# Attention by pairs of query tiles with transposed scores, on one Trainium2 core

## The chip, the cores and the metric

One NeuronCore of a Trainium2 chip runs one program. The metric is the device time of that program in microseconds (us). Engines are called as in the profile: PE (TensorE), PEld (its weight loads), DVE (VectorE), ACT (ScalarE), POOL (GpSimd), SP (SyncE).

## The reference

Two samples of 1024 tokens with 256 features, in two layers; x is (2, 1024, 256).

```
layer 0:  w[b]  = normalised(mix_weight * cond[b])             # 256x256 for each sample
          x     = x + tanh((w[b] mixed x) @ W @ A1 @ A2 + bias)
layer 1:  Q2 = x @ Wq2 + bq2;  K2 = x @ Wk2 + bk2;  V = [cond, x] @ Wv + bv
          A  = softmax(Q2 @ K2.T / 16) - alpha * softmax(constant rows)
          att = A @ V                                           # (2, 1024, 256)
          xq = fake_quant(att);  h = fake_quant(silu(xq @ Wg.T) * (xq @ Wu.T))
          x  = x + h @ Wd.T                                     # int8-like weights, I = 704
```

The second softmax has equal scores in each row, so the kernel replaces it by a rank-one term. `fake_quant` needs the largest magnitude of the whole attention output, so the FFN can't start before the last attention tile is done.

## The kernel before

All matmuls up to the attention are made of three fp32r passes over a high and a low half of each operand (`three_passes`, L1001): high by high, high by low, low by high. Every operand therefore exists as two tiles (`xh`/`xl` the projected queries, `x1h`/`x1l` the tokens that serve as keys, `vh`/`vl` the values, `pth`/`ptl` the probabilities). ACT writes the high half by a copy to fp32r, DVE or POOL the low half by a subtraction (`low`, L593).

The queries are projected by Wq2 Wk2^T at once, so scores are a product of `xh`/`xl` with the tokens themselves. The attention runs over 16 query tiles j of 128 queries (8 a sample). For each tile, in the order in which PE's program lists them (loop at L1247):

- `scores(j)`, L1127: queries on partitions, 1024 keys along two PSUM banks, 12 matmuls of 512 columns. Two pairs of banks alternate (0/1 and 2/3).
- `out_T(j-3)`, L1186: two transposes that bring an output tile back to feature-major form.
- `attend(j-2)`, L1155: 24 matmuls of 256 columns; the transposed probabilities are the weights, the values are the moving operand.
- single items of other work (`extra`, `do_extra`, L1212): 6 query projections of 6 matmuls each, 4 value tiles, transposes of the FFN weights.
- `prob_T(j-1)`, L1143: 8 transposes of 128x128, since the product with V needs keys on partitions.

Meanwhile DVE takes the row maximum of a tile (`row_max`, L733) and ACT makes the exponential straight from PSUM with the maximum as its bias and the row sum as its accumulator (`softmax`, L463). After `prob_T`, ACT copies the high half of the transposed tile (`probT_hi`, L473) and DVE makes the low half (`probT_lo`, L744). DVE scales the result by the reciprocal sum (`attention_out`, L750), PE transposes it back, ACT writes `outT` (`out_hi`, L480) and DVE takes its maximum (`out_max`, L759). POOL does no attention work; it quantises the FFN weights (L951 to L962), with scales that DVE makes in six turns (`ffn_weight_scales`, L764).

Before the loop PE runs 12 of the 16 value tiles with `scores(0)` and `scores(1)` between them (L1225), then `rank_columns` (L1237). PSUM bank 7 (`MISC`) is passed from item to item in the order of `misc_schedule` (L53); `misc_turn` (L1171) makes PE wait until the item before has been read. Every engine executes its program strictly in order. After the last tile PE waits for the maximum over all tiles and spreads it (`spread_max`, L1293, L1298), and the FFN begins.

Of the kernel before, what the change touches and what calls it, by code (L numbers as in the profile page):

```python
# [22 lines left out]
P = 128  # L23
# [8 lines left out]
NG = NH  # L32
IF = I // P
# [19 lines left out]
def misc_schedule():  # L53

    extra = {}
    for g in range(1, NG):  # L60
        for c in range(DC):
            extra[4 * (g - 1) + 1 + c] = [("query", g, c)]
    extra[1].insert(0, ("rank", 0))
    for j, v in ((3, 12), (4, 13), (7, 14), (8, 15)):
        extra[j] = [("value", v)]
    extra[11], extra[12], extra[13] = [("gate", 0)], [("gate", 1)], [("up", 0)]
    order = []
    for j in range(NT):
        if j >= 3:
            order.append(("out", j - 3))  # L70
        order += extra.get(j, [])

    order += [("out", NT - 3), ("out", NT - 2), ("out", NT - 1), ("down", 0), ("down", 1), ("up", 1)]
    return extra, order


def build_block(nc, x, cond, mix_w, l0_w, l0_a1, l0_a2, l0_bias, wq1, bq1, wq2, bq2, wk1, bk1, wk2, bk2,
                wv, bv, alpha, clip_x, clip_down, w_gate, w_up, w_down, out):
    extra, misc_order = misc_schedule()
    misc_at = {item: n for n, item in enumerate(misc_order)}  # L80

    def misc_reads(item):


        return sum(i[0] not in ("query", "value", "rank") for i in misc_order[:misc_at[item] + 1])
# [15 lines left out]
    def sums(u):  # L101
# [14 lines left out]
              (3, 4, "act", "act")]  # L116

# [8 lines left out]
    with ExitStack() as ctx:  # L126
# [42 lines left out]
        prob = sb("prob", [P, 2, L], F32)  # L169
        pth = sb("pth", [P, 2, TPB, P], F32R)  # L170
# [32 lines left out]
        with ExitStack() as scope:  # L203
# [4 lines left out]
            vh = sb("vh", [P, NT, D], F32R, scope)  # L208
            vl = sb("vl", [P, NT, D], F32R, scope)
# [5 lines left out]
            with ExitStack() as inner:  # L215
                ptl = sb("ptl", [P, 2, TPB, P], F32R, inner)
# [13 lines left out]
        MISC = 7  # L230
        own_bank = {("out", NT - 1): 6, ("down", 0): 4, ("down", 1): 5, ("up", 1): 7}

        def attended(j):
            return ps[:, 6, (j % 2) * D:(j % 2 + 1) * D] if j < NT - 1 else ps[:, 3, 0:D]

        def probT_bank(j, a):
            return a + (4 if j < NT - 1 else 0)

        EARLY_V = 12
# [49 lines left out]
        s_ps, nb_ready, p_ready = sem("s_ps"), sem("nb_ready"), sem("p_ready")  # L289
        t_ps, pth_ready, ptl_ready = sem("t_ps"), sem("pth_ready"), sem("ptl_ready")  # L290
# [29 lines left out]
        def hidden(u):  # L320
            i, t = units[u]
            return hid[:, i, t:t + L] if i < IF else hidr[:]

# [51 lines left out]
        def _(act):  # L375
# [75 lines left out]
            def query_hi(g, c, src):  # L451
                act.activation(xh[:, g // 2, c, half(g)], src, ACT.Identity, bias=col("ucol", c)).then_inc(qh_ready, 1)
# [7 lines left out]
            def value_hi(v, bank):  # L460
                copy(vh[:, v, :], ps[:, bank, 0:D], vh_ready)

            def softmax(j):  # L463
                act.wait_ge(nb_ready, j + 1)
                if j >= 2:
                    act.wait_ge(t_ps, 2 * (j - 1))
                if j >= 4:
                    act.wait_ge(o_ready, j - 3)
                act.activation(prob[:, j % 2, :], ps[:, 2 * (j % 2):2 * (j % 2) + 2, :], ACT.Exp,  # L469
                               bias=col("nb", j % 2), scale=ATT_SCALE,  # L470
                               accum_out=col("ls", j % 4)).then_inc(p_ready, 1)

            def probT_hi(j):  # L473
                for a in range(2):
                    act.wait_ge(t_ps, 2 * j + a + 1)
                    if j >= 2:
                        act.wait_ge(o_ps, j - 1)
                    copy(pth[:, j % 2, a * 4:(a + 1) * 4, :], ps[:, probT_bank(j, a), :], pth_ready)

            def out_hi(j):  # L480
# [916 lines left out]
```

## Time and profile before

| | |
|---|---|
| median of 3 runs | 244.15 us (243.93 to 244.63) |
| the profiled execution | 243.51 us, span 241.4 us, granted clock 0.983 |
| busy, share of the span | PE 94%, PEld 77%, DVE 63%, ACT 50%, POOL 29% |
| chain that ended last | PE 77%, DVE 13%, issue 3%, DMA 3%, ACT 2%, POOL 1% |
| attention stage | 57 to 191 us of the span |
| FFN and output | 191 to 241 us of the span |

The span runs from the first to the last instruction; 2.1 us of the profiled execution lie around it. Busy shares are averages over stages with different limits. Matmuls overlap, so the time that one costs is read from the starts of two neighbours and not from its duration. A granted clock of 1.0 is TensorE's 2.4 GHz, 0.5 is 1.2 GHz.

### The profile page before, as it was taken

The page shows a single profiled execution, that of the slowest core. Times are in us where ns is not written, and L with a number is a line of the kernel's source. Part 1 is how long each engine was busy: PE and PEld are TensorE (multiplying, and loading weights), DVE is VectorE, ACT ScalarE, POOL GpSimd, SP SyncE. Part 2 cuts the span into 40 slices and gives each one's busy share as a digit, 9 for nine tenths or more (in the row PEclk, how much of TensorE's full clock was granted, in tenths as well). Part 3 has the DMA queues.
Part 4 walks back from the last instruction along what each step waited for, and adds up shares of the span by engine and source line. Part 5 has one row for each costly group of instructions (what it writes and reads, how often), then busy time and mean ns, then how long its engine had stood idle before and what let it go on. Part 6 is the DMA issues. An engine that isn't in the chain of part 4 may idle for free.

```text
span 241.4 us, 3860 instructions
## 1 busy us (share of the span) xinstructions
PE 227.7 (94%) x1447; PEld 185.2 (77%) x1447; DVE 152.8 (63%) x328; ACT 120.9 (50%) x218; POOL 69.5 (29%) x95
## 2 busy tenths in 40 slices
PE   7379899999999999999999999999999999998994
PEld 7169799988997999989999998889999644433342
DVE  0772434687475568756876566455556497999963
ACT  2517442675334434443444534555436669944932
POOL 5265240433000000380572500000000065673750
PEclk9959999999999999999999999999999999999998
DMA  5980006600000000000000000000000000000044
GB/s 149 380 298 3 0 0 181 204 1 0 3 0 0 3 0 0 3 1 1 3 0 0 3 0 0 3 1 0 3 0 1 3 0 0 3 0 0 0 170 177
DMA packets 6817, 9.61 MB, mean 40 GB/s; under 512 B 768, under 2 KB 4880, under 8 KB 6800
## 3 DMA queue, kind: packets, MB, share of 16 engines
q1 hardware_dynamic: 6192, 8.59, 10.5%
q10 hardware_dynamic: 288, 0.79, 0.9%
q8 instruction: 11, 0.18, 0.3%
q0 software_dynamic: 320, 0.01, 0.1%
q14 instruction: 6, 0.05, 0.1%
HBM read 7.28 MB, written 2.10 MB: 39 GB/s over the span
## 4 chain that ended last, share of the span: by engine, by line
PE 77%; DVE 13%; issue 3%; DMA 3%; ACT 2%; POOL 1%; DVEq 0%; POOLq 0%
PE ps L1007 53%; PE ps L1151 6%; DVE hmax L851 4%; PE ps L1334 3%; PE ps L991 3%; DMA wl<-in_L_cond_weight 3%; PE ps L1286 2%; DVE hid L846 2%; PE ps L1036 1%; PE ps L1191 1%; PE ps L1360 1%; PE ps L999 1%; DVE wmix L622 1%; POOL hid L970 1%; DVE hi L893 1%
## 5 line engine op out<-in xcount | busy, mean ns | idle before, releaser
L1007 PE MATMUL ps<-vh,pth 128*128 128x256 f32 x128 | 37.4, 292 | 0.3 <-DVE ptl L594 0.3
L1007 PE MATMUL ps<-vl,pth 128*128 128x256 f32 x128 | 36.1, 282 | 0.0
L1007 PE MATMUL ps<-vh,ptl 128*128 128x256 f32 x128 | 36.1, 282 | 0.0
L469 ACT ACTIVATE prob<-ps,small 128x1024 f32<-128x1024 f32 x16 | 17.8, 1115 | 21.7 <-DVE small L741 21.7
L484 ACT ACTIVATE outT<-ps,small 128x128 f32<-128x128 f32 x32 | 10.0, 366 | 33.3 <-PE ps L1191 33.3
L1007 PE MATMUL ps<-x1h,xh 128*128 128x512 f32 x64 | 26.2, 409 | 0.0
L739 DVE TENSOR_REDUCE small<-ps 128x1 f32<-128x1024 f32 x16 | 19.6, 1222 | 10.1 <-PE ps L1007 9.9
L1007 PE MATMUL ps<-x1h,xl 128*128 128x512 f32 x64 | 25.2, 393 | 0.0
L1007 PEld LDWEIGHTS ps<-vh,pth 128*128 128x128 f32 x128 | 24.4, 191 | 0.9 <-issue 0.9
L1007 PE MATMUL ps<-x1l,xh 128*128 128x512 f32 x64 | 25.0, 390 | 0.0
L1007 PEld LDWEIGHTS ps<-vl,pth 128*128 128x128 f32 x128 | 24.5, 191 | 0.0
L1007 PEld LDWEIGHTS ps<-vh,ptl 128*128 128x128 f32 x128 | 24.4, 191 | 0.0
L594 DVE TENSOR_TENSOR ptl<-ps,pth 128x512 fp32r<-128x512 f32 x32 | 20.3, 679 | 4.6 <-ACT pth L383 4.6
L966 POOL CAST xq<-xi 128x512 bf16<-128x512 int8 x5 | 3.7, 774 | 57.4 <-DVE xi L830 57.4
L756 DVE TENSOR_SCALAR on_s<-ps,small 128x256 f32<-128x256 f32 x16 | 7.8, 485 | 18.2 <-issue 14.3
L383 ACT ACTIVATE pth<-ps 128x512 fp32r<-128x512 f32 x32 | 17.2, 598 | 1.4 <-PE ps L1151 1.2
L943 POOL TENSOR_TENSOR x1l<-x1T,x1h 128x512 fp32r<-128x512 f32 x8 | 10.1, 1280 | 25.4 <-ACT x1h L383 25.4
L1151 PE MATMUL ps<-ident,prob 128*128 128x128 f32 x128 | 16.6, 274 | 0.0
L1151 PEld LDWEIGHTS ps<-ident,prob 128*128 128x128 f32 x128 | 14.5, 141 | 0.8
L958 POOL TENSOR_SCALAR wgn<-wgn,winv 128x256 f32<-128x256 f32 x6 | 2.9, 479 | 39.5 <-DVE winv L772 39.5
L1007 PEld LDWEIGHTS ps<-x1h,xl 128*128 128x128 f32 x64 | 12.0, 188 | 2.7
L541 ACT ACTIVATE sil<-ps,gus 128x1024 f32<-128x1024 f32 (+1 forms) x12 | 12.4, 1046 | 3.1 <-PE ps L1286 3.1
(224 smaller groups left out, 549.9 us busy)
## 6 DMA issues: line engine op xcount, KB each, us to landing
result<-yst SPq DMA_DIRECT2D x8, 256.0 KB, 2.1
xn<-in_x SPq DMA_DIRECT2D x3, 512.0 KB, 8.8
wdn<-in_L_ffn_w_down SPq DMA_DIRECT2D x1, 704.0 KB, 7.4
wgn<-in_L_ffn_w_gate SPq DMA_DIRECT2D x1, 640.0 KB, 4.4
wun<-in_L_ffn_w_up SPq DMA_DIRECT2D x1, 640.0 KB, 5.3
xn<-in_x ACTq DMA_DIRECT2D x1, 512.0 KB, 8.4
a<-in_L_ffn_aux_weight SPq DMA_DIRECT2D x2, 256.0 KB, 8.6
wvf<-in_L_cond_Wv SPq DMA_DIRECT2D x1, 512.0 KB, 9.4
```

The lines of the kernel that those rows point to most:

```text
L383: act.activation(dst, src, ACT.Copy).then_inc(ready, 1)
L469: act.activation(prob[:, j % 2, :], ps[:, 2 * (j % 2):2 * (j % 2) + 2, :], ACT.Exp, bias=col("nb", j % 2), scale=ATT_SCALE, accum_out=col( ...
L484: ins = act.activation(outT[:, c, j * P:(j + 1) * P], ps[:, own_bank.get(("out", j), MISC), c * P:(c + 1) * P], ACT.Identity, bias=col("rc ...
L541: act.activation(sil[:, u % 4, s], flat(ps[:, 4 * (u % 2):4 * (u % 2) + 2, :])[:, s], ACT.Silu, scale=gus[:, units[u][0]:units[u][0] + 1]) ...
L594: dve.tensor_tensor(dst, src, hi.bitcast(F32), ALU.subtract).then_inc(ready, 1)
L739: link(dve.tensor_reduce(col("mx", j % 2), flat(ps[:, 2 * (j % 2):2 * (j % 2) + 2, :]), X_AXIS, ALU.max))
L756: dve.tensor_scalar(on_s[:, j % 2, :], attended(j), col("rl", j % 2), None, ALU.mult).then_inc(o_ready, 1)
L851: dve.tensor_reduce(hmax[:, u:u + 1], hidden(u), X_AXIS, ALU.max, apply_absolute_value=True).then_inc(hm_ready, 1)
L943: pool.tensor_tensor(x1l[:, n // 2, c, half(n)], x1T[:, n, c, :], x1h[:, n // 2, c, half(n)].bitcast(F32), ALU.subtract).then_inc(x1l_read ...
L991: last = pe.matmul(ps[:, bank, m * D:(m + 1) * D], aT[:, k, m * P:(m + 1) * P], b[:, k, :], start=(k == 0), stop=(k == DC - 1))
L1007: last = pe.matmul(dst, a, b, start=(n == 0), stop=(n == len(passes) - 1))
L1151: last = pe.transpose(ps[:, probT_bank(j, a), k * P:(k + 1) * P], prob[:, j % 2, (4 * a + k) * P:(4 * a + k + 1) * P], ident[:])
```

## The change

Query tiles are taken in 8 pairs g of 256 queries, and the scores are computed transposed.

- PE: `scores(g)` has keys on partitions. For each of 8 key tiles, 6 matmuls with the tokens as weights and 256 queries as columns; banks 0 to 3 hold one pair. There is no second set of banks, so each bank waits for the reader of the pair before. `prob_T` is gone. The values carry two columns of ones, so `attend` has 258 columns and yields the sum of the probabilities itself.
- The maximum of a query lies now across partitions and banks: DVE reduces over key tiles (`key_max`, two reductions that read PSUM in steps of 256 elements, and one maximum), PE transposes the result (`key_max_T`), DVE finishes it (`query_max`), and PE spreads it over all partitions (`spread_top`). Both PE steps stand inside `attend(g-1)`, ahead of its matmul 15 of the first tile and matmul 3 of the second.
- `distances(g)`: DVE subtracts the maximum from the scores in four pieces of 512 into `prob`, of which there is one only. ACT makes the exponential in place and then copies the high half, piece by piece. POOL makes the low halves of pieces 0 to 2, DVE that of piece 3; in the last pair POOL makes piece 0 and DVE the others.
- All 16 values, `rank_columns` and the first query projection stand before `scores(1)`. The output of a pair is transposed by four transposes (`out_T`) in the middle of `scores(g+2)`.
- The FFN weights are scaled by DVE in pairs 1 to 3, quantised by POOL after its low halves, and transposed by PE in pairs 4 to 6 and ahead of the last `attend`.

The core of the diff (all else in it is renaming, semaphores and the split of POOL's weight loop):

```diff
+QP = 256
+NP = TOK // QP
+PPB = L // QP
...
+            after_scores[2 * (g - 1) + c] = ("query", g, c)
+    after_attend = {4: ("gate", 0), 5: ("gate", 1), 6: ("up", 0)}
+    order = [("rank", 0), after_scores[0], after_scores[1]]
+    for g in range(2, NP):
+        order.append(("out", g - 2))
+        order += [t[g] for t in (after_scores, after_attend) if g in t]
+    at_end = [("up", 1), ("out", NP - 2), ("down", 0), ("down", 1), ("tile", 0), ("tile", 1)]
+    return after_scores, after_attend, at_end, order + at_end
...
+    def low_half_on(g, k):
+        return "dve" if k == 3 or (g == NP - 1 and k > 0) else "pool"
...
-        prob = sb("prob", [P, 2, L], F32)
-        pth = sb("pth", [P, 2, TPB, P], F32R)
+        prob = sb("prob", [P, TPB, QP], F32)
+        pth0 = sb("pth0", [P, TPB, QP], F32R)
...
+                ptl = sb("ptl", [P, 2, TPB, QP], F32R, inner)
+        pth = [pth0, xh[:, 1].rearrange("p c n -> p (c n)").rearrange("p (k q) -> p k q", k=TPB)]
+        maxima = downT.rearrange("p i d -> p (i d)").bitcast(F32)
+        kmax = maxima[:, 0:2 * QP].rearrange("p (h q) -> p h q", h=2)
+        qmax = maxima[:, 2 * QP:3 * QP]
...
-        EARLY_V = 12
+        MISC, MAXB = 7, 6
+        own_bank = {("up", 1): 1, ("down", 0): 2, ("down", 1): 3, ("tile", 0): MAXB, ("tile", 1): 0}
+        def value_bank(v):
+            return (6, 7, 4, 5)[v] if v < 4 else (5, 7, 4)[v % 3]
...
+            def softmax(g):
+                for k in range(4):
+                    act.wait_ge(d_ready, 4 * g + k + 1)
+                    act.activation(prob[:, 2 * k:2 * k + 2, :], prob[:, 2 * k:2 * k + 2, :], ACT.Exp,
+                                   scale=ATT_SCALE).then_inc(p_ready, 1)
+                    if k == 0 and g >= 2:
+                        act.wait_ge(o_ps, 2 * (g - 1))
+                    act.wait_ge(p_ready, 4 * g + k + 1)
+                    copy(pth[g % 2][:, 2 * k:2 * k + 2, :], prob[:, 2 * k:2 * k + 2, :], pth_ready)
...
+            for v in range(NT):
                 act.wait_ge(v_ps, v + 1)
...
+                value_hi(v, value_bank(v))
+            extra_read(after_scores[0])
+            softmax(0)
+            extra_read(after_scores[1])
             softmax(1)
...
+            for g in range(2, NP):
+                extra_read(("out", g - 2))
+                if g in after_scores:
+                    extra_read(after_scores[g])
+                softmax(g)
+                if g in after_attend:
+                    extra_read(after_attend[g])
             act.activation(col("junk"), ones[:, 0:1], ACT.Silu)
...
+            for item in at_end:
+                extra_read(item)
...
+            def key_max(g, h):
+                dve.wait_ge(s_ps, 2 * g + h + 1)
+                ins = dve.tensor_reduce(kmax[:, h, :], flat(ps[:, 2 * h:2 * h + 2, :]).rearrange("p (k q) -> p q k", k=4),
+                                        X_AXIS, ALU.max)
+                if h:
+                    link(ins)
+                    dve.tensor_tensor(kmax[:, 0, :], kmax[:, 0, :], kmax[:, 1, :], ALU.max).then_inc(kmax_ready, 1)
+            def query_max(g):
+                t = tcol[:, 2 * g:2 * g + 2]
+                dve.wait_ge(kmaxT_ps, g + 1)
+                link(dve.tensor_reduce(col("mx", 0, 2), ps[:, MAXB, 0:QP].rearrange("p (t k) -> p t k", t=2), X_AXIS,
+                                       ALU.max))
+                link(dve.tensor_tensor(col("m2", 0, 2), col("mx", 0, 2), t, ALU.add))
+                dve.tensor_tensor(col("nb", 0, 2), col("m2", 0, 2), t, ALU.subtract).then_inc(top_ready, 1)
+            def distances(g):
+                dve.wait_ge(top_ps, g + 1)
+                link(dve.tensor_copy(qmax, ps[:, MAXB, QP:2 * QP]))
+                for k in range(4):
+                    if g >= 1:
+                        e = low_half_on(g - 1, k)
+                        dve.wait_ge(ptl_ready[e], low_halves(g - 1, k, e))
+                    dve.tensor_tensor(prob[:, 2 * k:2 * k + 2, :], ps[:, k, :].rearrange("p (k q) -> p k q", k=2),
+                                      qmax.unsqueeze(1).broadcast_to([P, 2, QP]), ALU.subtract).then_inc(d_ready, 1)
+            def prob_lo(g):
+                for k in range(4):
+                    if low_half_on(g, k) == "dve":
+                        dve.wait_ge(pth_ready, 4 * g + k + 1)
+                        low(ptl[:, g % 2, 2 * k:2 * k + 2, :], prob[:, 2 * k:2 * k + 2, :],
+                            pth[g % 2][:, 2 * k:2 * k + 2, :], ptl_ready["dve"])
+            def attention_out(g, tiles=(0, 1)):
+                dve.wait_ge(o_ps, 2 * g + tiles[-1] + 1)
+                for t in tiles:
+                    link(dve.reciprocal(col("rl", t), ps[:, 4 + t, D:D + 1]))
+                if g >= 1:
+                    dve.wait_ge(misc_ps, misc_at[("out", g - 1)] + 1)
+                for t in tiles:
+                    dve.tensor_scalar(on_s[:, t, :], ps[:, 4 + t, 0:D], col("rl", t), None,
+                                      ALU.mult).then_inc(o_ready, 1)
...
+            for v in range(NT):
+                if v == 4:
+                    key_max(0, 0)
+                    key_max(0, 1)
+                value_lo(v, value_bank(v))
                 if v == 7:
                     rank_one_vectors()
+                if v == 9:
+                    dve.wait_ge(vl_ready, 2)
+                    query_max(0)
...
+            distances(0)
+            extra_lo(after_scores[0])
+            key_max(1, 0)
+            prob_lo(0)
+            dve.wait_ge(vl_ready, NT)
+            for g in range(1, NP):
+                if g >= 2:
+                    key_max(g, 0)
+                key_max(g, 1)
+                if g in after_scores:
+                    extra_lo(after_scores[g])
+                query_max(g)
+                distances(g)
+                if g < NP - 1:
+                    attention_out(g - 1)
+                    prob_lo(g)
+                    if g >= 2:
+                        out_max(("out", g - 2))
+                    if g <= 3:
+                        ffn_weight_scales(g - 1, 0)
+                        ffn_weight_scales(g - 1, 1)
+                else:
+                    prob_lo(g)
+                    attention_out(g - 1)
+                    out_max(("out", g - 2))
+            attention_out(NP - 1, (0,))
+            out_max(("out", NP - 2))
+            attention_out(NP - 1, (1,))
+            for t in range(2):
+                out_max(("tile", t))
...
+            def prob_lo(g):
+                for k in range(4):
+                    if low_half_on(g, k) == "pool":
+                        pool.wait_ge(pth_ready, 4 * g + k + 1)
+                        pool.tensor_tensor(ptl[:, g % 2, 2 * k:2 * k + 2, :], prob[:, 2 * k:2 * k + 2, :],
+                                           pth[g % 2][:, 2 * k:2 * k + 2, :].bitcast(F32),
+                                           ALU.subtract).then_inc(ptl_ready["pool"], 1)
+            for g in range(NP):
+                prob_lo(g)
+                if 1 <= g < NP - 1:
+                    k, part = (g - 1) // 2, (g - 1) % 2
+                    n = (IC if k < 2 else DC) // 2
+                    ffn_weight(k, range(part * n, (part + 1) * n))
...
+            def scores(g, midway=None):
+                b = g // PPB
+                pe.wait_ge(ql_ready, DC * (g // 2 + 1))
+                pe.wait_ge(x1l_ready, DC * 2 * (b + 1))
+                if g == 0:
                     pe.wait_ge(tanh_ready, DC * NH)
...
+                for k in range(TPB):
+                    if g >= 1 and k % 2 == 0:
+                        pe.wait_ge(d_ready, 4 * (g - 1) + k // 2 + 1)
+                    if midway and k == 4:
+                        midway()
+                    t = slice(k * P, (k + 1) * P)
+                    last = three_passes(ps[:, k // 2, k % 2 * QP:(k % 2 + 1) * QP],
+                                        [(x1h[:, b, c, t], x1l[:, b, c, t], queries(xh, g, c), queries(xl, g, c))
+                                         for c in range(DC)])
+                    if k % 4 == 3:
+                        last.then_inc(s_ps, 1)
+            def key_max_T(g):
+                pe.wait_ge(kmax_ready, g + 1)
+                for t in range(2):
+                    last = pe.transpose(ps[:, MAXB, t * P:(t + 1) * P], kmax[:, 0, t * P:(t + 1) * P], ident[:])
+                last.then_inc(kmaxT_ps, 1)
+            def spread_top(g):
+                pe.wait_ge(top_ready, g + 1)
+                for t in range(2):
+                    last = pe.transpose(ps[:, MAXB, QP + t * P:QP + (t + 1) * P], col("nb", t).broadcast_to([P, P]),
+                                        ident[:])
+                last.then_inc(top_ps, 1)
+            def attend(g, also=None):
+                b = g // PPB
+                if g == 0:
+                    pe.wait_ge(vl_ready, NT)
+                    pe.wait_ge(ones_ready, 3)
+                for t in range(2):
+                    if g >= 1:
+                        pe.wait_ge(o_ready, 2 * (g - 1) + t + 1)
+                    def before(n):
+                        if t == 0 and n % 6 == 0:
+                            e = low_half_on(g, n // 6)
+                            pe.wait_ge(ptl_ready[e], low_halves(g, n // 6, e))
+                        if also and (t, n) in also:
+                            also[(t, n)]()
+                    q = slice(t * P, (t + 1) * P)
+                    three_passes(ps[:, 4 + t, 0:VW],
+                                 [(pth[g % 2][:, k, q], ptl[:, g % 2, k, q], vh[:, b * TPB + k, :], vl[:, b * TPB + k, :])
+                                  for k in range(TPB)], before).then_inc(o_ps, 1)
...
+            values(range(4))
+            scores(0)
+            values(range(4, 9))
+            key_max_T(0)
+            values(range(9, 13))
+            spread_top(0)
+            values(range(13, NT))
+            do_extra(("rank", 0))
+            do_extra(after_scores[0])
+            for g in range(1, NP):
+                scores(g, (lambda: do_extra(("out", g - 2))) if g >= 2 else None)
+                if g in after_scores:
+                    do_extra(after_scores[g])
+                attend(g - 1, {(0, 15): lambda: key_max_T(g), (1, 3): lambda: spread_top(g)})
+                if g in after_attend:
+                    do_extra(after_attend[g])
+            for item in at_end[:-2]:
+                do_extra(item)
+            attend(NP - 1, {(1, 12): lambda: do_extra(("tile", 0))})
+            do_extra(("tile", 1))
```

## Rows read from the trace of the kernel before

**Rows 1.** The page, part 1: busy time of PE, share of the span, instructions.

```profile
PE 227.7 (94%) x1447; PEld 185.2 (77%) x1447; DVE 152.8 (63%) x328; ACT 120.9 (50%) x218; POOL 69.5 (29%) x95
```

**Rows 2.** Waits of PE: who waited for whom, us in total, times, longest.

```profile
PE ps L984 <- DMA a<-in_L_ffn_aux_weight: 4.0, 1, 4.0
...
PE ps L1191 <- DVE on_s L756: 0.4, 1, 0.4
PE ps L1007 <- DVE ptl L594: 0.3, 1, 0.3
```

**Rows 3.** The chain that ended last, one query tile: start us, us, what.

```profile
171.08 2.87 PE ps L1007 x24
173.95 0.87 PE ps L1151 x8
174.82 2.77 PE ps L1007 x12
177.59 0.22 PE ps L1191 x2
```

**Rows 4.** Timeline of PE: neighbours of 512 and of 256 columns; start us, us.

```profile
84.21 0.40 PE L1007 MATMUL ps<-x1h,xl 128*128 128x512 f32 x1
84.45 0.40 PE L1007 MATMUL ps<-x1h,xh 128*128 128x512 f32 x1
...
88.40 0.28 PE L1007 MATMUL ps<-vh,ptl 128*128 128x256 f32 x1
88.52 0.28 PE L1007 MATMUL ps<-vh,pth 128*128 128x256 f32 x1
```

**Rows 5.** Groups of DVE with shapes apart: xcount, busy us, mean ns, idle before.

```profile
L594 DVE TENSOR_TENSOR ptl<-ps,pth 128x512 fp32r<-128x512 f32 x32 | 20.3, 679 | 4.6 <-ACT pth L383 4.6
L739 DVE TENSOR_REDUCE small<-ps 128x1 f32<-128x1024 f32 x16 | 19.6, 1222 | 10.1 <-PE ps L1007 9.9
...
L756 DVE TENSOR_SCALAR on_s<-ps,small 128x256 f32<-128x256 f32 x16 | 7.8, 485 | 18.2 <-issue 14.3 <-PE ps L1007 2.2 <-DVE small L752 1.6
...
L594 DVE TENSOR_TENSOR vl<-ps,vh 128x256 fp32r<-128x256 f32 x16 | 6.6, 415 | 0.0
L761 DVE TENSOR_REDUCE amax<-outT 128x1 f32<-128x256 f32 x16 | 6.6, 410 | 0.8 <-ACT outT L484 0.8
L718 DVE SCALAR_TENSOR_TENSOR xl<-ps,small,xh 128x512 fp32r<-128x512 f32 x8 | 5.9, 750 | 10.2 <-ACT xh L452 10.1
...
L730 DVE TENSOR_SCALAR tcol<-ps,small 128x1 f32<-128x1 f32 x16 | 3.4, 215 | 6.4 <-ACT vh L383 6.4
...
L769 DVE TENSOR_REDUCE wmax<-wgn 128x3 f32<-128x768 f32 x2 | 1.9, 944 | 0.0
```

**Rows 6.** Groups of ACT and POOL, the same view.

```profile
L484 ACT ACTIVATE outT<-ps,small 128x128 f32<-128x128 f32 x32 | 10.0, 366 | 33.3 <-PE ps L1191 33.3
...
L383 ACT ACTIVATE x1h<-x1T 128x512 fp32r<-128x512 f32 x8 | 5.0, 627 | 1.3 <-DVE x1T L642 1.3
...
L502 ACT ACTIVATE gateT<-ps 128x704 bf16<-128x704 bf16 x2 | 1.5, 757 | 1.2 <-PE ps L1201 1.2
...
L943 POOL TENSOR_TENSOR x1l<-x1T,x1h 128x512 fp32r<-128x512 f32 x8 | 10.1, 1280 | 25.4 <-ACT x1h L383 25.4
```

**Rows 7.** Timeline at the end of attention: four copies and four subtractions in a row.

```profile
181.15 2.06 ACT L383 ACTIVATE pth<-ps 128x512 fp32r<-128x512 f32 x4 [0.61 <-PE ps L1151]
181.78 2.48 DVE L594 TENSOR_TENSOR ptl<-ps,pth 128x512 fp32r<-128x512 f32 x4 [0.52 <-ACT pth L383]
```

**Rows 8.** Stretches near the start: us; PE, PEld, DVE, ACT, POOL busy; clock; DMA.

```profile
11.00:12.00 1.00, 0.85 (x5) 0.45 (x4) 1.00 (x1) 0.94 (x2) 1.00 (x1) 0.59 1.09 387
...
17.50:18.00 0.50, 0.50 (x3) 0.41 (x2) 0.00 (x0) 0.00 (x0) 0.00 (x0) 0.50 0.11 27
18.00:18.50 0.50, 0.50 (x4) 0.45 (x4) 0.00 (x0) 0.00 (x0) 0.00 (x0) 1.00 0.04 5
```

**Rows 9.** Timeline of PE: the spread of the maximum, which ends the attention.

```profile
191.25 0.32 PE L1295 MATMUL ps<-ident,small 128*128 128x128 f32 x1
```

More of the change, by code:

```diff
@@ L116, in build_block, with low_halves @@
               (3, 4, "act", "act")]
+    def low_half_on(g, k):
+        return "dve" if k == 3 or (g == NP - 1 and k > 0) else "pool"
+    def low_halves(g, k, engine):
+        return sum(low_half_on(i, j) == engine for i in range(g + 1) for j in range(4) if (i, j) <= (g, k))
     def rounded_upto(piece, engine):
@@ L460, in value_hi @@
             def value_hi(v, bank):
[L461 to L480, printed above, removed]
-                act.wait_ge(misc_ps, misc_at[("out", j)] + 1)
+                copy(vh[:, v, 0:D], ps[:, bank, 0:D], vh_ready)
+            def softmax(g):
[7 more added lines that the diff above has]
+                    copy(pth[g % 2][:, 2 * k:2 * k + 2, :], prob[:, 2 * k:2 * k + 2, :], pth_ready)
@@ L491, in extra_read @@
                     query_hi(item[1], item[2], ps[:, MISC, :])
-                elif item[0] == "value":
-                    value_hi(item[1], MISC)
+                elif item[0] in ("out", "tile"):
+                    out_hi(item)
                 else:
@@ L954, in _ @@
                     pool.wait_ge(w8_ready, IC)
-                for i in range(IC if k < 2 else DC):
+                for i in rows:
                     j = k * IC + i
@@ L1184, in misc_turn, with out_T @@
                     pe.wait_ge(misc_used, misc_reads((kind, *at_)))
-            def out_T(j):
-                if ("out", j) not in own_bank:
-                    misc_turn(("out", j))
-                pe.wait_ge(o_ready, j + 1)
-                for c in range(DC):
-                    last = pe.transpose(ps[:, own_bank.get(("out", j), MISC), c * P:(c + 1) * P], on_s[:, j % 2, c * P:(c + 1) * P], ident[:])
-                last.then_inc(misc_ps, 1)
+            def out_T(item):
+                kind, n = item
+                g, tiles = (n, (0, 1)) if kind == "out" else (NP - 1, (n,))
+                pe.wait_ge(o_ready, 2 * g + tiles[-1] + 1)
+                for m, t in enumerate(tiles):
+                    for c in range(DC):
+                        at_col = m * D + c * P
+                        last = pe.transpose(ps[:, own_bank.get(item, MISC), at_col:at_col + P],
+                                            on_s[:, t, c * P:(c + 1) * P], ident[:])
+                return last
             def ffn_weight_T(kind, c):
@@ L1212, in do_extra @@
             def do_extra(item):
-                if own_bank.get(item, MISC) == MISC:
+                if item not in own_bank:
                     misc_turn(item)
+                elif item[0] in ("up", "down"):
+                    pe.wait_ge(d_ready, 4 * (NP - 1) + own_bank[item] + 1)
                 if item[0] == "query":
                     last = query(item[1], item[2], MISC)
-                elif item[0] == "value":
-                    last = value(item[1], MISC)
+                elif item[0] in ("out", "tile"):
+                    last = out_T(item)
                 elif item[0] == "rank":
```

242 lines of the change are left out of this document (52 added, 190 removed).

## The prediction, made before the changed kernel was built

> **What bounds the kernel now.** I read the page first: PE is busy 227.7 of 241.4 us [rows 1]. Busy alone proves little for matmuls, so the waits come next: from the values to the end of attention PE waits 0.3 us once for a low half and 0.4 us once for an output tile, and for little else [rows 2]. The chain that ended last then gives the make-up of a query tile: 2.87 us attend, 0.87 prob_T, 2.77 scores, 0.22 out_T, 6.73 in all with no piece of another engine [rows 3]. So in this stage PE's stream sets the time, and DVE, ACT and POOL are hidden behind it. Two questions decide the change: how much of PE's stream goes, and whether the others stay hidden.
>
> **PE's work.** The price of a matmul is the distance between two starts: 0.24 us or a little less at 512 columns (2.77/12 = 0.231), 0.12 us at 256 [rows 3, 4]. An fp32 transpose is 0.87/8 = 0.109, two of them 0.22 [rows 3].
> - prob_T goes: 16 x 0.87 = 13.9 us saved.
> - Scores of a pair: 48 x 0.12 = 5.74 in place of 2 x 2.77 = 5.54, so 8 x 0.2 = +1.6. That a load of weights for every 256 columns stays hidden is shown by attend, which has just that form.
> - key_max_T and spread_top: 4 transposes a pair, 8 x 0.44 = +3.5.
> - Two more columns in 384 matmuls: below 1 ns each, +0.3.
> - Values, projections, weight transposes and out_T only move.
>
> Net -8.5 us. That is what the change is worth if nothing waits.
>
> **What the others get.** DVE prices [rows 5]: reduction of 1024, 1.22; subtraction of 512 from PSUM, 0.68, or 0.60 each in a row (2.48 for four [rows 7]); scaling of 256, 0.49; maximum of 256, 0.42 (as the subtraction of 256); query low half 0.75; a scale turn 0.94 + 2 x 0.18 = 1.3. ACT: exponential or copy of 512 from SBUF 0.63; two that depend on each other 1.19 a piece, as the next piece may start 0.1 before the last has ended [rows 6, 7]. POOL: low half of 512, 1.28 [rows 6], three a pair, hidden. A PE result reaches another engine some 0.25 us after the slot of its last matmul.
>
> Let T be the start of attend(g-1) on PE. key_max's second half runs T+0.25 to 1.47, the maximum is ready at 1.96; PE wants it at 15 x 0.12 = 1.80. spread_top is due at 3.6 and can be had at 3.5. The four distances are ready at 5.3, 5.9, 6.5, 7.1; ACT's eight operations fill 5.3 to 10.1; the last low half is ready at 10.9. attend(g) starts at T+12.4 (13.8 with a projection). In mid-run the long chain fits. It fails in these places:
>
> a) **Before the loop.** Both key_max reductions stand ahead of value_lo(4), and values 7 and 11 wait for DVE: 0.4. From the end of scores(0) PE has 12 values of 0.72 (6 x 0.12) and two pairs of transposes, with that wait 9.5 us. DVE has the second reduction and maximum, 1.7; 12 low values of 0.54 (0.215 + 0.415 less overlap, [rows 5]), 6.5; rank-one vectors 0.9 and query_max 0.8 (small operations near 0.2 each, [rows 5]); and waits of some 0.9 for values that come late: 10.8. So rank_columns waits 1.3 for the last value. The projection then waits 0.6 for rcol. Before, all these had work between them. Together +2.3.
>
> b) **The maximum, pairs 2 to 4.** There DVE has two scale turns (2.6) before key_max. Lo at 10.9, out_max 0.65, scales to 14.2, two key_max and the maximum to 16.5 (in pair 2 less, without out_max). PE wants it at 13.8 + 1.8 = 15.6. Waits 0.5, 1.1, 1.1, and 0.16 in two others: +2.9.
>
> c) **Bank 7 in pairs 5 to 7.** ACT reads the transposed gate or up weights after its whole softmax: 10.1 + 0.76 [rows 6] = T+10.9. PE wants bank 7 for out_T in the middle of the next scores, at 6.4 + 0.5 (gate transposes) + 2.9 = 9.8. Three waits of 1.15: +3.5.
>
> d) **The last pair.** out_T(6) and attend(7) need attention_out(6). On DVE this stands behind prob_lo(7), whose last piece ends at T+10.9; the reciprocals and two scalings bring 12.1. PE is free at T+6.9, as nothing is left but up. A hole of 5.3 us, +5.3. Before, prob_T and out_T filled this place.
>
> e) **The end chain.** attend, on_s, tile_T, out_hi, out_max, the maximum over tiles: 0.3 + 0.5 + 0.2 us up to the last transposes and 0.3 + 0.7 + 0.4 + 0.2 behind them, 2.5 of waits, where the kernel before waits 0.4 [rows 2], since weight transposes lay there: +2.1.
>
> f) **The clock.** Near the start PE idles 4.0 us [rows 2]; after that the granted clock falls from 1.0 to 0.5 (1.2 GHz) in the stretch 11 to 12 and is back only at 18.0 [rows 8]. The hole of d) is longer, so I expect the same. It stayed low for 6.8 us (11.2, from the mean of 0.59 in that stretch, to 18.0). Between 0 (no drop) and 3.4 (half of 6.8, had PE worked all through) I take 2.2, two thirds, as part of the low time falls into the hole itself, where it costs nothing.
>
> Small moved work costs nothing more: POOL's weight loop has 3.9 us a pair beside 3.8 of low halves in a period of 12.4 or more, and gate, up and down are quantised a pair before PE asks. A low half on DVE may start 0.1 later behind one of POOL's. If that cover went, each us would join b) or d).
>
> **Sum.** -8.5 + 2.3 + 2.9 + 3.5 + 5.3 + 2.1 = +7.6, less the 0.3 that PE waited for the first low half before [rows 2], +7.3; plus 2.2 for the clock, +9.5. PE then spreads the maximum at 191.25 + 9.5 = 200.8 [rows 9], and what follows is untouched. The profiled execution would be 243.5 + 9.5 = 253.0; it lies 0.6 below the median of its runs. Either figure is within my rounding, so I give 253.0.
>
> **The unknown price.** key_max reads PSUM in steps of 256 elements, and no row shows such a reading. Lower bound: the same count and memory in line, 1.22. Upper: the widest ratio that rows show for one job on two ways of access, POOL over DVE for 512 elements, 1.28/0.68 [rows 5, 6], so 2.3. I take 1.22, as the nearest row is the same instruction on the same banks.
>
> The Trainium skill, Vector Engine (DVE) Microarchitecture Reference, section Measured stream behaviour on trn2, speaks against the change here: an SBUF source that hops on every element ran at 1.73 ns an element where a contiguous one ran at 1.05. It has no row for PSUM. Were it to hold, an estimate by that page is 1.9 us for a reduction and about 6 us more in the sum; no trace here shows it.
>
> **Rivals.**
> 1. *Forecast: slower through waits, 253.0.* For it: the program orders in a) to e) are fixed and their prices are rows. Without the clock drop it is 250.8. Together 0.58.
> 2. *Steps through PSUM are dear.* At the middle of the bounds, 1.76, each second reduction puts 0.54 on PE's path in 7 pairs (3.8), again 0.54 in two pairs with scales and in the prologue (1.1): +4.9, 257.9; at 2.3 it is +10. This is the case to which the page's rule leads. Against it: nothing in the trace. 0.25.
> 3. *Faster: the softmax chain is short enough.* It decides at ACT's pieces. If one took 0.65 us and not 1.19, the softmax would end at T+7.9 and the last low half at 8.7. Then b) falls to 0.2 (-2.7), c) goes (-3.5), d) shrinks to 3.1 (-2.2), less than the idle time that did lower the clock, which would stay up (-2.2): 9.5 - 10.6 = -1.1, or 242.4. For it: ACT is idle half of the span [rows 1], and four copies from PSUM do run at 0.5 apiece [rows 7]. Against: 0.63 from SBUF is a row [rows 6], a piece has two operations, and each copy waits for its own exponential. The point of no loss is near 0.8. 0.12.
> 4. *No change.* The 8.5 saved and the waits cancel: rival 3 with pieces of about 0.8, 244. The measurement can tell 0.3% (0.7 us) from no change. 0.05.
>
> That the change doesn't do what it says (transposes of probabilities left, or a weight load that no longer hides) would show as a busy PE with no waits and a later end; the 0.12 us of attend, whose weights also change every 256 columns, speaks against it [rows 3, 4].
>
> So slower 0.83, same 0.05, faster 0.12. The range takes in rivals 1 and 2 up to a price near 2.1 and the lower waits: 246 to 261.
>
> **What would show it.** PE's matmuls of scores 0.12 us apart and 128 transposes fewer; PE waiting 5 us on on_s before out_T, with a clock of 0.5 after it; three waits of about 1.1 in the middle of scores on ACT; a key_max group with a mean of 1.22. A mean near 1.9 is rival 2. Exp and copy groups well below 0.63 and no wait in mid-scores would be rival 3. I am wrong in the main point if PE's waits from 57 us to the spread are below 8 us together.

## The result, and the profile after

The changed kernel takes 260.4 us (median of 4 executions, 257.5 to 260.6) against 244.4 us of the kernel before beside it: a ratio of 1.063, interval 1.059 to 1.067. It is slower, as forecast (253.0, range 246 to 261), and by more than the forecast. The granted clock differs from one execution of the same program to the next, and times differ with it, so below each kernel also has **span times mean granted clock**, the span with the time at half clock counted as half, as if PE's stream set the time all through it. It is 243.2 us for the changed kernel (4 executions, 241.6 to 244.5) and 237.2 for the kernel before (23 executions, 236.3 to 237.7).

The profiled execution: 260.6 us, span 258.8, clock 0.940; before 243.5, 241.4 and 0.983. First the page of the changed kernel, busy time of each engine:

```profile
PE 232.7 (90%) x1543; PEld 195.5 (76%) x1543; DVE 166.8 (64%) x341; ACT 120.5 (47%) x204; POOL 99.5 (38%) x117
```

PE has 4 points less than in [rows 1]: it waits now. Its stretches by windows (us, PE busy, clock, DMA share, GB/s):

```profile
0.00:36.30 36.30, 29.65 (x170) 0.86 0.44 138
36.30:43.10 6.80, 6.80 (x34) 0.50 0.47 127
43.10:60.56 17.46, 17.46 (x105) 1.00 0.26 84
60.56:206.93 146.37, 132.08 (x1019) 0.97 0.00 1
206.93:258.80 51.87, 46.72 (x220) 0.96 0.11 41
```

The values start at 60.56, the maximum is spread at 206.93. The kernel before has 56.88 and 191.25 for the same points. So of the 17.4 us by which the span is longer, 3.7 lie ahead of the values, in code that is unchanged; 12.0 in the attention (146.4 for 134.4); 1.7 behind it. Who made PE wait, in the changed kernel (total, times, longest):

```profile
PE ps L1245 <- DVE on_s L778: 6.0, 2, 5.2
PE ps L1030 <- DMA a<-in_L_ffn_aux_weight: 3.2, 1, 3.2
PE ps L1245 <- issue: 2.6, 3, 0.9
PE ps L1194 <- DVE downT L742: 2.5, 3, 1.3
...
PE ps L1349 <- DVE small L851: 1.4, 1, 1.4
...
PE ps L1299 <- DVE vl L592: 1.1, 1, 1.1
```

Each wait of the forecast has a row: d) and part of e) (`on_s`, 5.2 and 0.8), c) (three of 0.9, put down to "issue"), b) (`kmax`, which shares memory with `downT`), the rest of e) (1.4), and a) (1.1, with 0.4 for `rcol` beside it). With 0.2 that the kernel before has too, they come to 14.2 us in this stage, where the kernel before has 0.9 [rows 2].

The chain that ended last shows the middle of the scores of pair 7 (start us, us, what):

```profile
171.03 2.52 PE ps L1053 x21
173.55 0.43 PE ps L1256 x6
173.97 3.07 PE ps L1053 x24
177.04 0.86 issue
177.91 0.63 PE ps L1245 x4
178.53 4.66 PE ps L1053 x39
183.19 0.42 PE ps L1194 x2
```

The second row is the transposed up weights, the fourth the wait until ACT has read them. The stream is 0.12 us a matmul as forecast (2.52/21, 4.66/39), but the 24 ahead of the wait take 3.07 and not 2.87. The timeline of PE shows why, first four output transposes inside a stream, then four behind the wait:

```profile
131.58 0.28 PE L1053 MATMUL ps<-xh,x1l 128*128 128x256 f32 x1
131.71 0.60 PE L1245 MATMUL ps<-ident,on_s 128*128 128x128 f32 x4
132.06 0.36 PE L1053 MATMUL ps<-xh,x1h 128*128 128x256 f32 x1
...
176.76 0.28 PE L1053 MATMUL ps<-xh,x1l 128*128 128x256 f32 x1
177.91 0.63 PE L1245 MATMUL ps<-ident,on_s 128*128 128x128 f32 x4 [0.86 <-issue]
178.29 0.36 PE L1053 MATMUL ps<-xh,x1h 128*128 128x256 f32 x1
```

In a stream the next instruction starts 0.13 us after a matmul. Ahead of a wait the matmul's whole 0.28 passes before the idle time is counted. So a wait costs PE almost 0.2 us more than its row says (1.15 + 0.38 from start to start, where the stream has 0.13 + 0.35: 1.05 for a row of 0.86). The switch from matmuls to these transposes costs nothing by itself.

The last pair in the timeline, where the hole is (the stretch in which PE stands still):

```profile
190.77 0.63 ACT L392 ACTIVATE xh<-prob 128x512 fp32r<-128x512 f32 x1
191.42 1.28 ACT L526 ACT_TABLE_LOAD   x1
191.43 0.69 DVE L592 TENSOR_TENSOR ptl<-prob,xh 128x512 fp32r<-128x512 f32 x1 [0.49 <-ACT xh L392]
192.04 0.36 DVE L774 RECIPROCAL small<-ps 128x1 f32<-128x1 f32 x2
192.44 0.88 DVE L778 TENSOR_SCALAR on_s<-ps,small 128x256 f32<-128x256 f32 x2
...
193.46 1.09 PE L1245 MATMUL ps<-ident,on_s 128*128 128x128 f32 x4 [5.24 <-DVE on_s L778]
```

The scaling of pair 6, whose product had been ready for 4.2 us (PE's last matmul of it ended at 187.80), stands on DVE behind the last low half of pair 7; that waits for ACT's eighth operation. And the four stretches in which the clock is low beyond those of the kernel before (same columns as above):

```profile
36.30:43.10 6.80, 6.80 (x34) 0.50 0.47 127
84.20:87.30 3.10, 3.10 (x15) 0.50 0.02 5
193.30:200.10 6.80, 6.64 (x35) 0.50 0.00 0
206.90:210.30 3.40, 3.37 (x9) 0.51 0.00 0
```

At half speed they lose 3.4, 1.6, 3.4 and 1.7 if PE's stream sets the time there, together 10 of the 17.4 us at most. The fall near the start is longer as well: the mean clock from 9.0 to 19.5 us is 0.51, and 0.67 in the kernel before, another 1.7 us at most. With 1.1 us less of waiting near the start (3.2 and 1.3 for 4.0 and 1.6) that accounts for the 3.7 us ahead of the values: they come from the clock and not from the order of the attention. Last, the groups of DVE, ACT and POOL that answer to [rows 5, 6]:

```profile
L761 DVE TENSOR_TENSOR prob<-ps,downT 128x512 f32<-128x512 f32 x32 | 19.9, 683 | 0.3
L738 DVE TENSOR_REDUCE downT<-ps 128x256 f32<-128x1024 f32 x16 | 19.2, 1215 | 11.9 <-PE ps L1053 11.9
...
L475 ACT ACTIVATE prob<-prob 128x512 f32<-128x512 f32 x32 | 19.8, 619 | 38.2 <-DVE prob L761 38.2
...
L999 POOL TENSOR_TENSOR ptl<-prob,pth 128x512 fp32r<-128x512 f32 x12 | 15.2, 1292 | 38.9 <-ACT pth L392 38.9
```

`key_max`, which steps through PSUM, has a mean of 1.215 us where the contiguous reduction has 1.222 [rows 5]: the steps cost nothing.

### The profile page after: what moved, and what is told of

Same layout as the page of the kernel before. It is cut to its first block, busy times and chain, and to the rows that moved or that the text cites. A ratio compares the mean times of both kernels' runs of the same rounds, so it can differ in the third digit from the quotient of the medians.

```text
span 258.8 us, 3975 instructions
## 1 busy us (share of the span) xinstructions
PE 232.7 (90%) x1543; PEld 195.5 (76%) x1543; DVE 166.8 (64%) x341; ACT 120.5 (47%) x204; POOL 99.5 (38%) x117
## 4 chain that ended last, share of the span: by engine, by line
PE 61%; DVE 22%; ACT 9%; issue 3%; DMA 2%; POOL 1%; ACTq 0%; DVEq 0%; POOLq 0%
PE ps L1053 40%; ACT prob L475 3%; DVE hmax L881 3%; DVE downT L738 3%; ACT xh L392 3%; PE ps L1037 3%; PE ps L1388 3%; DMA wl<-in_L_cond_weight 2%; DVE wmax L793 2%; PE ps L1045 2%; PE ps L1340 2%; DVE hid L876 1%; PE ps L1245 1%; PE ps L1082 1%; DVE ptl L592 1%
## 5 line engine op out<-in xcount | busy, mean ns | idle before, releaser
L1053 PE MATMUL ps<-xh,x1h 128*128 128x256 f32 x128 | 37.6, 294 | 0.0
L475 ACT ACTIVATE prob<-prob 128x512 f32<-128x512 f32 x32 | 19.8, 619 | 38.2 <-DVE prob L761 38.2
L1053 PE MATMUL ps<-vh,ptl 128*128 128x258 f32 x128 | 36.9, 288 | 0.0
L1053 PE MATMUL ps<-xl,x1h 128*128 128x256 f32 x128 | 36.8, 288 | 0.0
L1053 PE MATMUL ps<-xh,x1l 128*128 128x256 f32 x128 | 36.8, 287 | 0.0
L1053 PEld LDWEIGHTS ps<-xh,x1h 128*128 128x128 f32 x128 | 25.1, 196 | 0.2
L1053 PEld LDWEIGHTS ps<-xl,x1h 128*128 128x128 f32 x128 | 25.2, 197 | 0.1
L1053 PEld LDWEIGHTS ps<-xh,x1l 128*128 128x128 f32 x128 | 25.1, 196 | 0.0
L761 DVE TENSOR_TENSOR prob<-ps,downT 128x512 f32<-128x512 f32 x32 | 19.9, 683 | 0.3
L1053 PE MATMUL ps<-vh,xh 128*128 128x258 f32 x64 | 19.7, 307 | 0.0
```

What stands on the lines that cost most here:

```text
L475: act.activation(prob[:, 2 * k:2 * k + 2, :], prob[:, 2 * k:2 * k + 2, :], ACT.Exp, scale=ATT_SCALE).then_inc(p_ready, 1)
L761: dve.tensor_tensor(prob[:, 2 * k:2 * k + 2, :], ps[:, k, :].rearrange("p (k q) -> p k q", k=2), qmax.unsqueeze(1).broadcast_to([P, 2, QP] ...
L1053: last = pe.matmul(dst, a, b, start=(n == 0), stop=(n == len(passes) - 1))
```

## The experiments

All are edits of the changed kernel. In the expectations, theory W says that the time is lost in waits which the order of the programs sets; its rivals say that an engine is short of time, so that a wait only moves. The differences of span times clock below are against the control, 243.4, up to the three moves, and against the run before from there on. First one wait each.

**The last pair in another order.**

```diff
                 else:
-                    prob_lo(g)
                     attention_out(g - 1)
+                    prob_lo(g)
```

> One change to the changed kernel: in the last pair DVE scales the output of pair 6 before it makes its low halves, so PE gets on_s about 3.4 us earlier. Theory W (the time is lost in waits set by program order, plus the clock that the long hole lowers): the wait of 5.2 us before the output transposes shrinks to about 1.8, the clock stays at 1.0 afterwards, which gives back another 2.8; total about -6 us (254). Rival D (DVE and ACT are simply short of time there, the wait moves): the low halves come later by the 1.3 us of scalings and attend(7) waits for them; total -1 to -2.5 us, clock still falls.

Measured: 252.3 us median, ratio to the kernel before 1.020 [1.010, 1.030]; span times clock 240.2, 3.2 less than the 243.4 of the control below. The interval leaves open whether it is 2% slower than the kernel before. PE's waits for `on_s`:

```profile
PE ps L1245 <- DVE on_s L778: 2.1, 2, 1.4
```

The 5.2 became 1.4 (6.0 to 2.1 in total), no other wait came up, and in the profiled execution the clock stayed at 1.0 from 186 to 200; theory W holds. The expected 6 us were counted from 260.4, which gave 254; the median is 1.7 below that, but only 4.6 below the control's 256.9.

**Dummy work in the hole.**

```diff
             for item in at_end[:-2]:
+                if item[0] == "out":
+                    pe.wait_ge(d_ready, 4 * (NP - 1) + 1)
+                    keep_warm(0, 24)
                 do_extra(item)
```

> One change to the changed kernel: 24 dummy matmuls of 512 bf16 columns (5.2 us of PE) in the hole before the output transposes of pair 6. They do nothing for the wait itself, so this prices the clock alone. Theory W: on_s comes at the same moment, the clock stays at 1.0 through attend(7), total -2.8 us and perhaps 1.5 more if the later fall near the start of the FFN goes too. Rival: the clock after the hole costs nothing as PE has slack there: no change.

Measured: 253.4 us, ratio 1.038 [1.030, 1.046], 3.5 below the control. In the timeline the transposes follow the dummies, and their four take 0.63, not 1.09:

```profile
188.04 5.35 PE L1045 MATMUL ps<-gateT,identb 128*128 128x512 bf16 x24
193.35 0.63 PE L1245 MATMUL ps<-ident,on_s 128*128 128x128 f32 x4
```

Nothing in the work or the waits was shortened, and in this profile the clock is 1.0 from 193 to 211. What that is worth shows best inside the profiles. The spread of the maximum, in the changed kernel and here:

```profile
206.93 0.46 PE L1349 MATMUL ps<-ident,small 128*128 128x128 f32 x1 [1.42 <-DVE small L851]
203.93 0.32 PE L1352 MATMUL ps<-ident,small 128*128 128x128 f32 x1 [1.42 <-DVE small L851]
```

From the output transposes to this spread it is 13.5 us in the changed kernel (193.46 to 206.93) and 10.6 here (193.35 to 203.93), with the same waits: 2.9 us for the clock behind the hole, as W expected (2.8). The control, below, has 13.1, and the two runs after this one, which have the hole too, 12.9 and 12.8; the run before, without it, 10.6. So the price of the hole's clock was 2.2 to 2.9 us, by how much of the low time fell into the hole. The 3.5 us between the medians are no such clean price, as the clock elsewhere differs from execution to execution and the two intervals overlap. Span times clock is 244.9 here, 1.5 above the control, though no work was added in PE's way. So that measure is itself good to some 1.5 us only, and below it the rows of the waits decide.

**ACT reads the weights in the middle of its softmax.**

```diff
                 for k in range(4):
+                    if k == 2 and read:
+                        extra_read(read)
...
-                softmax(g)
-                if g in after_attend:
-                    extra_read(after_attend[g])
+                softmax(g, after_attend.get(g))
```

> One change to the changed kernel: in pairs 4 to 6 ACT reads the transposed gate and up weights between the second and the third piece of its softmax, not behind the fourth. Theory W: the three waits of 0.86 us in mid-scores go, nothing takes their place: -2.6 us. Rival D: the softmax ends 0.7 us later each time, the low halves with it, and the wait moves to attend or to the next maximum: 0 to -1 us.

Measured: 252.4 us, ratio 1.031 [1.021, 1.040]; span times clock 240.9, so -2.5. PE's waits have no "issue" row any more:

```profile
PE ps L1245 <- DVE on_s L778: 6.0, 2, 5.2
PE ps L1030 <- DMA a<-in_L_ffn_aux_weight: 2.6, 1, 2.6
PE ps L1194 <- DVE downT L742: 2.6, 3, 1.3
```

The 2.6 us are gone, and none came back in the other waits. So it was ACT's late reading that PE waited for in the rows put down to "issue".

**One turn of scales in each of pairs 1 to 6.**

```diff
-                    if g <= 3:
-                        ffn_weight_scales(g - 1, 0)
-                        ffn_weight_scales(g - 1, 1)
+                    ffn_weight_scales((g - 1) // 2, (g - 1) % 2)
...
-                pool.wait_ge(winv_ready, 2 * (k + 1))
+                pool.wait_ge(winv_ready, 2 * k + (1 if rows[0] == 0 else 2))
```

> One change to the changed kernel: DVE makes one turn of weight scales in each of pairs 1 to 6 in place of two in pairs 1 to 3 (POOL waits for the half that it needs). Theory W: the waits for the maximum in pairs 2 to 4 (1.3 us at most, 2.5 together) go: -2 to -2.5 us. Rival D: each turn delays key_max of its pair by the same 1.3 us spread wider, three new waits of some 0.5 us: 0 to -1 us.

Measured: 255.3 us, ratio 1.032 [1.025, 1.039]; span times clock 240.5, so -2.9. The row of `downT` is gone from PE's waits, and no new one came. Its clock was low by draw (mean 0.950 over four executions), which is why the median tells less here than the product.

**Control: the changed kernel again.**

> The changed kernel itself once more, five rounds. Theory W with a clock that falls at different places from execution to execution: the time varies with the mean granted clock, from about 252 (clock 0.965) to 260.5 (0.94), while span times clock stays near 243; so the median of 260.4 was a draw of low clocks. Rival (the clock of 0.94 belongs to this program): all executions again near 260 at 0.94.

Measured: 256.9 us (6 executions, 254.1 to 260.4), ratio 1.047 [1.040, 1.055]; clocks of 0.945 to 0.966, span times clock 243.4. So of the first 16.0 us, some 3.5 were a draw of low clocks; of the 12.3 that are left, about half (6.1) is there with the clock taken out. In this profile the clock is low in other places, and for longer near the rank columns:

```profile
38.10:41.50 3.40, 3.40 (x20) 0.55 0.93 273
78.60:85.50 6.90, 6.46 (x26) 0.51 0.01 2
191.30:198.10 6.80, 5.85 (x31) 0.50 0.00 0
205.00:208.40 3.40, 3.04 (x8) 0.50 0.00 0
```

**The three moves of order together.**

> The three moves of order of the runs before together on the changed kernel: output of pair 6 scaled before the last low halves, weights read in mid-softmax, one turn of scales a pair. Theory W (independent waits): their savings in span times clock add, 3.2 + 2.3 + 2.6 = 8.1 from 243.3 to about 235.2, against 236.9 of the kernel before; with clocks of 0.965 to 0.98 a time of 242 to 246, about that of the kernel before. Rival D (the slack is one and the same): savings overlap, span times clock stays at 238 or above, time 247 or more.

Measured: 247.6 us, ratio 1.006 [1.001, 1.011]; span times clock 236.7 (12 executions). The three savings alone come to 3.2 + 2.5 + 2.9 = 8.6, together they are 6.7. What is missing has a row, the first of these two:

```profile
PE ps L1192 <- DVE downT L742: 2.3, 2, 1.2
PE ps L1243 <- DVE on_s L778: 2.1, 2, 1.4
```

These two waits for the maximum, at 165 and 179 us, are in the last pairs, where the period has no projection and each scale turn and mid-softmax read falls into it. Neither edit alone made them. W's "independent" was wrong by about 2 us; the larger part adds.

**The rank columns earlier.** Added to the three moves: `misc_turn` waits for `vl_ready` of `NT - 2` for its first item.

> As the run with the three moves, and rank_columns waits for 14 of 16 low values (those whose bank it takes), not for all. Theory W: the wait of 1.1 us before it shrinks to near 0: -0.8 to -1.1 us of span times clock, and perhaps the clock no longer falls near 84 us, another -1.5. Rival: the wait moves to the query projection, which needs rcol from DVE behind the same low values: no change.

Measured: 244.4 us, ratio 0.997 [0.993, 1.002]; span times clock 235.7, so -1.0. No difference from the kernel before can be told. The wait for `vl` is gone, which confirms the 1.0 by a row, and in the profiled execution the clock does not fall near 84. The rest of the 3.2 us between this median and that of the three moves is, by the same measure, the clock.

**The kernel before, one look.**

> The kernel before, one profiled look, to see where its clock falls in an execution of 0.964 if one is met: theory W expects the same place as in the changed kernel, in the unchanged stretch near 33 to 43 us where PE runs 32 matmuls of one or two columns. At 0.978 only the fall near 11 to 18 us is seen.

Measured: 243.1 us at 0.982, with the fall near the start alone. No execution at 0.964 was profiled, so where its clock falls in those stays open. That there are such is in the 23 executions beside the runs: spans of 241.2 to 242.8 at 0.978 to 0.983, and of 244.8 to 245.2 at 0.964 to 0.971.

**Scales before the first low half.** Added to the run with the early rank columns: two turns of scales go in front of `prob_lo(0)` on DVE, one in each of pairs 1 to 4.

> On the kernel with three moves and the early rank: DVE makes the first two turns of weight scales before its first low half and one in each of pairs 1 to 4, none in pairs 5 and 6. There the period has no projection and the trace of the run before shows two waits of 1.2 us for the maximum. Theory W: both go, nothing takes their place: -2.3 us of span times clock, from 235.7 to about 233.4; at the same clocks a time near 242. Rival D: the two early turns hold up the first low half and with it attend(0): at most -1 us.

Measured: 242.0 us, ratio 0.987 [0.980, 0.994]; span times clock 234.1, so -1.6. The wait for `downT` is 0.6 in place of 2.3. The gain is less than the 2.3 expected: both late waits are gone, but one of 0.6 came in pair 1.

**Dummies at the end of attention.**

```diff
             for item in at_end[:-2]:
+                if item[0] == "out":
+                    pe.wait_ge(d_ready, 4 * (NP - 1) + 1)
+                    keep_warm(0, 5)
                 do_extra(item)
             attend(NP - 1, {(1, 12): lambda: do_extra(("tile", 0))})
+            keep_warm(4, 4)
             do_extra(("tile", 1))
+            keep_warm(4, 6)
```

> As the run before, with 15 dummy matmuls of 512 bf16 columns in the waits at the end of attention (5 before the output transposes of pair 6, 4 and 6 around those of the last tile), which price the clock at this place. Theory W: the waits are over at the same moment (within 0.3 us), the clock that fell near 190 us no longer does, -1.5 us where it would have; time near 240.5 to 241.5, below the kernel before (244.6). Rival: the fall comes from the two transposes themselves or costs nothing: no change, or +0.5 for dummies that end late.

Measured: 241.9 us (6 executions, 240.8 to 243.9), ratio 0.987 [0.980, 0.994]; span times clock 233.5. In the run before this one the clock was low twice near here:

```profile
183.40:186.80 3.40, 3.40 (x18) 0.53 0.00 0
193.30:196.60 3.30, 3.14 (x8) 0.52 0.00 0
```

With the dummies no such fall was seen in the profiled execution, but the medians of the two are the same, 242.0 and 241.9: a gain of the size expected is not shown. The two versions beat both kernels, the one before by 1.3% (0.6% to 2.0%).

**Where the clock fell, in all profiles.** Beside the fall near the start, which all twelve profiles have, the profiles of the changed kernel and its edits (ten) show falls at four places.

- Behind the rank columns (78 to 84 us): in all seven where PE waits there for `vl`, in none of the three without that wait. The 16 matmuls of two columns are in all ten.
- At the hole (from 185 to 193 us on): 6.8 us long in all four that have 5.2 us of idle PE, and in none of the six whose hole is shorter or filled.
- At the spread of the maximum: in six of ten. It is missing in the two runs with dummies, but also in two without any, so what the dummies do for it is not shown.
- Near 36 us: in eight of ten, and in neither of the two profiles of the kernel before.

## Why the prediction was right, and where its sizes were off

The sign and the mechanism held: PE's stream got shorter, and order on the other engines gave back more. That 260.4 lies inside the range is partly luck: the range reached to 261 for rival 2, which did not come, and the room was used up by falls of the clock that the sum did not have. By its own steps, in the profiled execution:

- **PE's work, -8.5: measured -6.3** (12.0, less 13.3 of added waits and 5.0 of clock). The price of 0.12 us held for scores and attend. What no term had is the 0.2 us that each wait costs beyond its row; this stage has 11 waits, which by that estimate makes the 2.2 us that are missing.
- **a) +2.3: 1.5.** The rank waited 1.1 and rcol 0.4 as forecast (1.3, 0.6); the value waits were too short to be listed.
- **b) +2.9: 2.5,** in the three pairs named (the waits at 109 and 124 us are 0.4 and 1.3); the two of 0.16 were not there. The working had a slip: from 14.2, two reductions and the maximum at its own prices end at 17.1 and not at 16.5, so the longest wait would have been 1.5; it was 1.3.
- **c) +3.5: 2.6,** three of 0.86 and not 1.15. The mechanism is shown by its removal (-2.5).
- **d) +5.3: 5.2,** and the reordering took 3.8 of it away (3.2 by span times clock).
- **e) 2.5 of waits: 2.2.**
- **f) the clock, +2.2: 10.** This is the step that failed. The fall at the hole came, and its price was right in kind and nearly in size: 2.9 in the profiled execution, 2.2 to 2.5 in three others. But I priced this one alone. I did not ask where else PE's stream had become thin: behind the wait for the rank columns (1.6), at the first FFN matmuls behind the end chain (1.7), and 3.4 in the unchanged stretch near 36 us, which no wait of this change explains. For the rank columns the ten profiles bear it out, as the fall goes when the wait goes; for the other two the cause is not shown. The control shows that part of this is chance: its median is 12.3 above that of the kernel before, not 16.0.

With the clock taken out the change costs 6.1 us (243.3, the mean of both sets, less 237.2), where my sum without the clock was 7.3.

**Rival 2** fell: 1.215 us. The rate in the Trainium skill (Vector Engine (DVE) Microarchitecture Reference, Measured stream behaviour on trn2) was taken in SBUF, from an operation with two sources, and the trace shows that it does not carry over to this read of PSUM by a reduction with one: by an estimate from it the group would have had a mean near 1.9. **Rival 3** fell: ACT's exponential takes 0.619 and its copy 0.632, as the row said. But its idea that the waits are what stands between this change and a gain was right: with four moves of order and no cheaper operation the kernel came out at 0.987 of the time before. That the cost was in the order, not in the transposed form, is shown by the runs above, in which the transposed form stays and only the order changes; I had put the chance of "faster" in the speed of ACT, and not looked at how little had to be moved.

Left open: what makes the clock fall near 36 us in some executions. No run changed that stretch.

## What to carry to other kernels

When a change makes one engine's stream shorter, walk each other engine's program in its order and ask of every item what it stands behind: here four items stood behind work that they did not need (a scaling, a read of weights, scale turns, the rank columns), and moving them turned +4.7% (the control) into -1.3%. Price the granted clock as well at every place where the stream of PE gets a hole or a run of tiny matmuls, and where executions draw different clocks, compare kernels by span times clock as well, down to the 1.5 us to which it can be trusted, and by the rows of the waits below that.

## What the runs showed of the hardware

- The same program ran at mean granted clocks of 0.940 to 0.966, and its time moved from 260.6 to 254.1 with it.
- The clock fell to 0.5 at 36.3 us in a stretch where the profile has PE busy throughout; PE had just run 24 of 32 matmuls of one or two columns in a row. In the control it fell at 37.6, 1.3 us behind the last of the 32. The same code in the kernel before kept 1.0 in its two profiled executions.
- In the hole the clock fell 5.1 us after PE had stopped in the changed kernel, just before it resumed; in the control 4.2 us after, and in the run with the read in mid-softmax 3.7 us after, in the middle of the hole. It stayed low for 6.8 us each time.
- A DVE subtraction of 512 with both inputs in SBUF took 0.69 us three times, in the last pair, and 0.84 seven times, in the other pairs. Those seven each start some 0.3 us before the last of POOL's low halves ends (the one at 102.86 for example, where POOL's end at 103.15); of the three, two have no POOL instruction beside them. That POOL is the cause is likely, but no run took it away. The tile view of `ptl` in the changed kernel (duration ns, min/median/max); the first row mixes both kinds:

```profile
L592 DVE TENSOR_TENSOR ptl<-prob,xh x6: 691/764/843, 102.9 to 191.4; 128x512 fp32r<-128x512 f32 x6
L592 DVE TENSOR_TENSOR ptl<-prob,pth x4: 828/836/845, 90.1 to 177.2; 128x512 fp32r<-128x512 f32 x4
```

- An interrupted PE stream costs almost 0.2 us more than the wait's row: 1.05 us for a row of 0.86, nearly all of it ahead of the wait, where the last matmul's 0.28 us count and not 0.13.
- `tensor_reduce` of 1024 from PSUM in steps of 256 elements took 1.215 us, in line 1.222.
